# Three bf16 parts of keys and queries in DRAM once, repeated by terms on the way back

## The reference, cut to what matters

```python
qh = _split_heads(q @ wq + bq)
kh = _split_heads(k @ wk + bk)
logits = jnp.einsum('bhqd,bhkd->bhqk', qh, kh) * scale
logits = logits + mask * -1000000000.0
attn = jax.nn.softmax(logits, axis=-1)
out = jnp.einsum('bhqk,bhkd->bhqd', attn, vh)
```

## Time and profile before

| | us |
|---|---|
| median of 3 runs | 693.57 (693.21 to 693.69) |
| the profiled execution's own time | 696.93 |
| its span | 695.5 |
| TensorE busy | 650.4 (94%) |
| VectorE busy | 521.2 (75%) |
| ScalarE busy | 400.8 (58%) |
| GpSimd busy | 412.1 (59%) |
| granted clock of TensorE | 0.999 of full |
| moved by DMA | 84.97 MB, of it 25.80 MB written to DRAM |

### The profile page before, as it was taken

One profiled execution on the slowest core, in us unless ns is written; L12 is line 12 of the kernel. 1 busy time (PEld: TensorE's weight loads), 2 busy tenths in 40 slices (PEclk: granted clock), 3 DMA queues, 4 the chain that ended last, 5 costly groups with the idle time before them and its releaser, 6 DMA issues.

```text
span 695.5 us, 14219 instructions
## 1 busy us (share of the span) xinstructions
PE 650.4 (94%) x5301; PEld 343.9 (49%) x5301; DVE 521.2 (75%) x934; ACT 400.8 (58%) x568; POOL 412.1 (59%) x613
## 2 busy tenths in 40 slices
PE   5989999999999999999999999999999999988997
PEld 3333443434343666666656643334434344455897
DVE  4798999999888783942654568898998988766554
ACT  2057777777778634233222257777787777754443
POOL 3444558667412255769954565967977744547445
PEclk9999999999999999999999999999999999999999
DMA  6836635742600576485862406546645545104411
GB/s 175 217 98 163 164 107 126 180 125 60 156 2 3 119 187 139 147 175 144 195 149 78 94 23 149 161 129 153 175 142 120 153 109 177 35 31 133 121 33 39
DMA packets 66601, 84.97 MB, mean 122 GB/s; under 512 B 7776, under 2 KB 48624, under 8 KB 65024
## 3 DMA queue, kind: packets, MB, share of 16 engines
q1 hardware_dynamic: 63856, 79.44, 44.4%
q0 software_dynamic: 1760, 3.62, 1.6%
q10 hardware_dynamic: 916, 1.00, 0.6%
HBM read 57.57 MB, written 25.80 MB: 120 GB/s over the span
## 4 chain that ended last, share of the span: by engine, by line
PE 64%; ACT 12%; DVE 6%; POOL 5%; DMA 5%; issue 4%; SPq 3%; ACTq 0%; DVEq 0%; POOLq 0%
PE pair L497 11%; ACT prob L919 11%; PE misc L510 7%; PE outs L510 6%; PE outs L624 6%; PE pair L458 6%; PE pair L358 5%; PE pair L360 4%; PE pair L359 4%; PE misc L411 3%; DVE negmax L1206 2%; PE outs L396 2%; DMA col<-in_L_b 2%; DMA qstack<-mT 1%; POOL hid L1870 1%
## 5 line engine op out<-in xcount | busy, mean ns | idle before, releaser
L1206 DVE TENSOR_REDUCE negmax<-pair 128x2 f32<-128x1024 f32 x256 | 306.6, 1213 | 37.6 <-PE pair L458 31.6
L919 ACT ACTIVATE prob<-pair 128x1024 f32<-128x1024 f32 x256 | 260.2, 1025 | 89.7 <-PE pair L497 85.3
L497 PE MATMUL pair<-qstack,kstack 54*128 54x256 bf16 x1024 | 100.4, 274 | 20.8 <-ACT prob L919 19.3
L458 PE MATMUL pair<-kstack,qstack 51*128 51x512 bf16 (+1 forms) x512 | 98.1, 379 | 1.6 <-DVE negmax L1206 0.8
L1440 DVE TENSOR_TENSOR hid<-pair,silu 128x512 f32<-128x512 f32 x68 | 46.7, 688 | 70.1 <-PE pair L360 51.3
L497 PEld LDWEIGHTS pair<-qstack,kstack 54*128 54x128 bf16 x1024 | 29.9, 94 | 126.0 <-ACT prob L919 101.1
L1066 ACT ACTIVATE silu<-pair 128x512 f32<-128x512 f32 x68 | 40.6, 599 | 88.6 <-PE pair L360 86.5
L510 PE MATMUL outs<-prob,vaug 128*32 128x256 f32 x1024 | 83.4, 390 | 0.0
L510 PE MATMUL misc<-prob,vaug 128*32 128x256 f32 x1024 | 81.0, 391 | 0.3
L624 PE MATMUL outs<-hid,down 128*128 128x512 f32 x136 | 70.3, 598 | 1.7 <-POOL hid L1870 1.6
L358 PE MATMUL pair<-xT,eh 128*128 128x512 f32 x136 | 70.3, 517 | 0.0
(11 more groups left out here) (290 smaller groups left out, 1086.4 us busy)
## 6 DMA issues: line engine op xcount, KB each, us to landing
kstack<-k_terms SPq DMA_DIRECT2D x30, 384.0 KB
w_here<-w_rows SPq DMA_DIRECT2D x32, 256.0 KB, 4.8
w_there<-w_rows SPq DMA_DIRECT2D x32, 256.0 KB, 5.1
k_terms<-kparts SPq DMA_DIRECT2D x16, 384.0 KB, 2.6
qstack<-q_terms SPq DMA_DIRECT2D x30, 192.0 KB, 4.3
ctx_nat<-in_ctxT SPq DMA_DIRECT2D x16, 256.0 KB, 3.2
k_terms<-kparts SPq DMA_DIRECT2D x16, 256.0 KB, 2.9
w_nat<-in_L_gu SPq DMA_DIRECT2D x9, 352.0 KB, 3.7
```

The source lines that it names most:

```text
L458: return nc.tensor.matmul(to, qstack[n % 3][rows, g, qt * P:(qt + 1) * P], kstack[n % 3][rows, g, :], start=True, stop=True)
L497: e = nc.tensor.matmul(bank[m + r][:, k * SQ:(k + 1) * SQ], kstack[n % 3][rows, g, (c + k) * P:(c + k + 1) * P], qstack[n % 3][rows, g, :] ...
L919: nc.scalar.activation(prob[:, quad % 2, 2 * g:2 * g + 2, c:c + 2, :].rearrange("p j c q -> p j (c q)"), pair[t_pair(n, step)][:, :, :], A ...
L1206: nc.vector.tensor_reduce(negmax[:, n % 2, 2 * g:2 * g + 2, qt], pair[score_pair(n, step)][:, :, :], AX.X, ALU.max, negate=True).then_inc( ...
```

## The change

Batches 0 and 1 stay as they were. From batch 2 on, each part is written to DRAM once (`k_parts`, `q_parts`): one transfer for k and one for q in place of three each, 384 KB in place of 768 KB for k, 192 KB in place of 384 KB for q. The repetition moves to the read: each half of a stack is read in three transfers, of 24, 16 and 8 rows (the runs of terms), so six transfers in place of two for k and six in place of two for q. For k a run of terms is parts 0 to 2, 0 to 1 or 0, which lie one behind the other in DRAM, and the source is a plain list of rows. For q a run is one part, repeated: the source has a first dimension of 3 or 2 with step 0, then 8 depths. The bytes read stay the same. The waits that count landings are adapted (`k_dmas`, `q_dmas`, `k_writes`, `q_writes`).

```diff
 def k_dmas(n):
-    return 16 * sum(4 if m < B else 2 for m in range(n % 3, n + 1, 3))
+    return 16 * sum((2 if m < 2 else 2 * len(RUNS)) + (2 if m < B else 0) for m in range(n % 3, n + 1, 3))

 def q_dmas(n):
-    return 16 * 2 * len(range(n % 3, n + 1, 3))
+    return 16 * sum(2 if m < 2 else 2 * len(RUNS) for m in range(n % 3, n + 1, 3))
+
+def k_writes(n):
+    return 16 * (len(RUNS) + n // 2) if n >= 0 else 0
+
+def q_writes(n):
+    return 16 * (len(RUNS) * min(n + 1, 2) + max(n - 1, 0))
...
+        k_parts = nc.dram_tensor("k_parts", (2, 3, P, SK), BF16, kind="Internal").ap()
+        q_parts = nc.dram_tensor("q_parts", (3, P, SQ), BF16, kind="Internal").ap()
...
-                    pool.wait_ge(k_out[n % 2], 48 * (n // 2))
+                    pool.wait_ge(k_out[n % 2], k_writes(n - 2))
...
-                    pool.wait_ge(q_out, 48 * n)
+                    pool.wait_ge(q_out, q_writes(n - 1))
...
                 if n >= 2:
                     sp.wait_ge(ld_k[(n - 2) % 3], k_dmas(n - 2))
+                    nc.sync.dma_start(k_parts[n % 2].rearrange("m p k -> p m k"), kparts[:, 0:3, n % 2, :]).then_inc(k_out[n % 2], 16)
+                    return
...
-                sp.wait_ge(k_out[n % 2], 48 * (n // 2 + 1))
+                sp.wait_ge(k_out[n % 2], k_writes(n))
                 for r in range(2):
...
+                    else:
+                        for _, first, terms in RUNS:
+                            rows = slice(HALF * r + HD * first, HALF * r + HD * (first + terms))
+                            nc.sync.dma_start(kstack[i][rows, :, :],
+                                              k_parts[n % 2, 0:terms].rearrange("m (d r g) k -> r (m d) (g k)", r=2, g=PAIRS)[r]).then_inc(ld_k[i], 16)
...
+                if n >= 2:
+                    nc.sync.dma_start(q_parts.rearrange("m p q -> p m q"), qparts[:, 0:3, :]).then_inc(q_out, 16)
+                    return
...
-                sp.wait_ge(q_out, 48 * (n + 1))
+                sp.wait_ge(q_out, q_writes(n))
                 for r in range(2):
...
+                    else:
+                        for part, first, terms in RUNS:
+                            rows = slice(HALF * r + HD * first, HALF * r + HD * (first + terms))
+                            nc.sync.dma_start(qstack[i][rows, :, :],
+                                              q_parts[part].rearrange("(d r g) q -> r d (g q)", r=2, g=PAIRS)[r]
+                                              .unsqueeze(0).to_broadcast([terms, HD, PAIRS * SQ])).then_inc(ld_q[i], 16)
```

More of the change, by code:

```diff
@@ L2023, in stack_k @@
                 sp.wait_ge(t_done, STEPS * (n - 2))
-                sp.wait_ge(k_out[n % 2], 48 * (n // 2 + 1))
+                sp.wait_ge(k_out[n % 2], k_writes(n))
                 for r in range(2):
-                    nc.sync.dma_start(kstack[i][HALF * r:HALF * r + MASK_ROW, :, :],
-                                      k_terms[n % 2].rearrange("m (d r g) k -> r (m d) (g k)", r=2, g=PAIRS)[r]).then_inc(ld_k[i], 16)
+                    if n < 2:
+                        nc.sync.dma_start(kstack[i][HALF * r:HALF * r + MASK_ROW, :, :],
+                                          k_terms[n % 2].rearrange("m (d r g) k -> r (m d) (g k)", r=2, g=PAIRS)[r]).then_inc(ld_k[i], 16)
+                    else:
[3 more added lines that the diff above has]
+                                              k_parts[n % 2, 0:terms].rearrange("m (d r g) k -> r (m d) (g k)", r=2, g=PAIRS)[r]).then_inc(ld_k[i], 16)
                 if n < B:
@@ L2064, in stack_q @@
                 sp.wait_ge(t_done, STEPS * (n - 2))
-                sp.wait_ge(q_out, 48 * (n + 1))
+                sp.wait_ge(q_out, q_writes(n))
                 for r in range(2):
-                    nc.sync.dma_start(qstack[i][HALF * r:HALF * r + MASK_ROW, :, :],
-                                      q_terms.rearrange("m (d r g) q -> r (m d) (g q)", r=2, g=PAIRS)[r]).then_inc(ld_q[i], 16)
+                    if n < 2:
+                        nc.sync.dma_start(qstack[i][HALF * r:HALF * r + MASK_ROW, :, :],
+                                          q_terms.rearrange("m (d r g) q -> r (m d) (g q)", r=2, g=PAIRS)[r]).then_inc(ld_q[i], 16)
+                    else:
[4 more added lines that the diff above has]
+                                              .unsqueeze(0).to_broadcast([terms, HD, PAIRS * SQ])).then_inc(ld_q[i], 16)
             def stack_max(n, half):
```

## The result

| | us |
|---|---|
| changed kernel, median of 4 runs | 776.81 (775.86 to 786.52) |
| kernel before, beside it on the same chip | 693.63 (693.21 to 695.08) |
| ratio | 1.1209 (95% interval 1.1173 to 1.1246) |
| span of the profiled execution | 775.1 (695.5 before) |
| mean granted clock of TensorE | 0.931 (0.999 before) |

Slower by 83 us. The prediction had the sign and the first cause, the few engines that carry q, and less than a quarter of the size.

What follows compares the result with a forecast made beforehand. The prediction took q's stack as last to arrive in both layers, delaying in-order TensorE one for one. Slower q reads less earlier reads and margins gave +19.2 us over twelve periods: 712.8 us from 693.57, range 695 to 735.

Steps and rivals of the forecast that it cites:

- The terms of q: Reads of q: busiest engine carries 139 KB in place of 25 KB, +4.6 us a period in layer 0, +4.5 in layer 1.
- Even spread: Rival, 7%: repeated source split by its 24 rows, q lands earlier, 692.0 us; decides up to 9 pieces more, 1.5 us.
- Compensated: Rival, 10%: few engines run above 24 GB/s and the k stage ends earlier than counted; 0 to +5, some 696 us.
- No such change: Rival that the writes are not halved; excluded, since SP's order shows one write for each of k and q.
- The sum: Twelve periods: +2.0 in 1 to 3, +1.2 in 0, 4, 5, +2.1 in 8 to 10, +1.1 in 11 to 13; +19.2 us.
- what would show it: Expected signs in the changed profile, among them TensorE idle 1 to 3 us before line 458 or 497 at twelve places.
- the term 4.5 - 2.4: Layer 1, periods 8 to 10: q's slower reads, 4.5 us, less 2.4 from earlier k reads and smaller q writes; +2.1 each.
- the 1.0 us of margin: Layer 1, periods 11 to 13: q's read lands at 508.9, 1.0 before 509.92, so only +1.1 us each.
- 2.6 us earlier: Layer 0, periods 1 to 3: one k write lands 3.0 us after issue, so SP reads k 2.6 us earlier.
- alone covered: Layer 0: SP's added issues delay the next maxima from 106.80 to 108.2, covered because the period begins at 113.84.
- k's own term: Reads of k: busiest engine gets 8 pieces of 8 KB in place of 6; up to 1.3 us, taken as nothing.
- Starved: Rival, 8%: the three engines stay at 12.9 GB/s and layer 1's exchanges wait behind them; over +40, about 745 us.

Runs made afterwards that it cites:

- e12_late_twice: Kernel before with its wide transfers; in periods 2 to 6 of layer 0 the maxima of half a stack copied twice more after landing: 733.91 us, 1.0313.
- e13_warm_fourteen: Changed kernel with 14 idle products ahead of step 0 of periods 1 to 6 of each layer: 765.72 us, 1.0764 times the kernel before.
- e10_warm_ten: Changed kernel with 10 idle products ahead of step 0 of periods 1 to 6 of each layer: 763.91 us, 1.0989 times the kernel before.
- e2_k_alone: Changed kernel with q put back as before, so only k is written once and read in runs: 703.92 us, 1.0106 times the kernel before.
- e5_q_runs_of_terms: Kernel before with its full writes, but each half of q read in three transfers of 24, 16 and 8 plain rows: ratio 1.0055.

## Why the prediction was wrong

*Right.* The three, two and eight engines, and that this decides; the bytes written (17.54 MB, about 17.5 predicted); the stretch in which two or three engines move 50 to 74 GB/s; q, or the maxima issued behind it, as the last thing to arrive. The terms of q, +4.6 in layer 0 and +4.5 in layer 1, measured +2.3 to +5.9 in the six periods of layer 0, 4.2 in the mean (periods 1, 2 and 4: 13.74, 12.46 and 11.73 us from the reads of q to the product, against 7.88, 7.86 and 6.56; the least, in period 5, 12.59 against 10.30), and +4.1 in period 8. The reads of k in layer 1 came 1.5 us earlier, as said. *Even spread*, *Compensated* and *No such change* are out.

*Wrong, the largest step, 33 us:* "The sum" took each period up to its write of k from the kernel before, and the part on what would show it had TensorE "idle 1 to 3 us" with nothing behind that. The idle time is not the whole price. Behind every wait of the changed kernel but the first, 2.0 us and more, the clock went to half. TensorE's steps came later by it, and with them the maxima of the running batch, behind which SP issues the write of k: 2.4 to 2.8 us late in layer 0, 2.0 to 3.7 in layer 1. `e12_late_twice` shows this with wide reads of q and k, and the periods of the runs with idle products in which the clock held show the narrow reads without it. The prediction itself says that the next period's transfers are timed from that period's own steps; the sum did not use it.

*Wrong, second step, layer 1, 25.8 us where the sum had 9.6:* the term 4.5 - 2.4. It took q's write 0.9 us earlier for the smaller traffic and left SP's four issues more for k out of that layer, though they stand ahead of q's write there. From k's reads to q's it became 1.7 us more (9.30 against 7.58): 1.3 by the issues, and 0.4 by q's write, whose smaller size brought nothing. Period 8 is thus at 4.1 - 1.5 + 1.7 = +4.3, not +2.1; the 1.0 us of margin that I gave periods 11 to 13 took nothing off (+4.3 to +4.7 too).

*Wrong, third step, layer 0, 21.4 us where the sum had 9.6:* "2.6 us earlier" for k, and SP's issues as "alone covered". The write landed 4.1 us after its issue (median of four) in place of the 3.0 of the earlier trace rows, so that the reads came 0.8 and 1.4 us earlier in periods 2 and 1, and 0.7 to 1.3 in the others. And k's issues do not only delay the maxima; they stand ahead of q's reads, +1.0. Why the write lands at 4.0 to 4.9 us in periods 0 to 3 and at 2.8 in 4 and 5 is open: the transfers that SP issues behind it are the same but for the context, absent in period 5. Half clock in the same period does not make it: period 1 of the changed kernel has it at the full clock, and period 1 of `e13_warm_fourteen`, with half clock from 71.5 to 78.5, has 2.8. But where idle products kept the waits short, k was read 2.8 us after its write from period 1 or 2 on, and in periods 2 and 3 of `e10_warm_ten` the way from the write to the product grew by 2.2 us, where the changed kernel has 4.8 and 3.4. So a part of the 21.4 is not the price of the narrow reads by itself.

*Smaller:* k's own term was taken as nothing, and `e2_k_alone` measured +7.5 us; it is a part of both layers' figures above. The six reads of q cost SP 3.7 to 3.8 us, not 3.2. And nine pieces more (the condition of *Even spread*) are 1.7 us at 21.5 GB/s, not 1.5.

The range's upper end of 735 had no case for the first step. *Starved* was nearer in size (over +40) for another reason, engines that stay at 12.9 GB/s, which the traces do not show: at 127 to 129.68 they moved some 24 to 27 GB/s each, and the exchanges, though late, were not what held the next stack.

## What to carry to other kernels

Count the engines of a transfer by its outermost dimension on both sides before counting its bytes: halving what is written is worth nothing if the read then comes from a source of 3 x 8 rows, and where a repetition can be had as runs of 16 plain rows it costs nothing. When a change makes TensorE wait, do not add only the wait: look at the granted clock behind the longest waits in the trace, and if it falls, price the next steps at half speed, and ask whether they feed the transfer that was late. Ask it of the list of the issuing engine too: here k's parts lay ready for over 12 us while SP stood before another transfer. Whether the write issued ahead of the maxima would have saved the 33 us, no run shows.

## What the runs showed of the hardware

- **The clock and waits.** Behind waits of 1.14, 1.22, 1.36, 1.60, 1.89, 2.08 and 2.14 us at the head of a period the granted clock stayed at 1.00; behind 1.42, 1.44, 1.75, 1.88 and 2.00 us, and behind 3.40 us too, it fell to 0.50 within about two microseconds; behind 2.40, 2.52, 2.67 and 4.90 us it had fallen already. Behind all waits of 2.2 us and more in the periods of these traces it fell; below that both happened. It then stayed at 0.50 for 7, 10 or, once, 14 us in the changed kernel, for 3.4 us at some places of `e10_warm_ten` and `e13_warm_fourteen`, though TensorE was busy (6.00 of the 6.00 us from 98 to 104). The Trainium skill ("TensorE: Matmul & The Clock Gate", "HAM oscillation — how this bites in real kernels") describes a kernel whose every tile waits for a DMA and starts slow; this trace agrees, with 0.60 to 0.61 us in place of 0.39 behind nine of its eleven waits of 2.0 us or more.
- **Work that saves time.** Twenty idle products at twelve places, 4.49 us each, made the changed kernel faster (1.0816 against 1.1136 to 1.1209 times the kernel before on the same chip, the chips being different ones).
- **Chips differ.** The kernel before took from 693.6 to 710.5 us on the five chips, more than `e2_k_alone` or `e5_q_runs_of_terms` differ from it. Without the run beside it neither could be read.
